# Two-layer message passing on a graph: dense rows moved out of the first 14 steps of stage one, and three node types packed into one number

## What is computed

```python
h = jnp.maximum(_layernorm(x, axis=-1), 0.0)
gate = jax.nn.silu(edge_attr @ W1.T + b1) @ W2.T + b2
ei = emb[atom_z[src]]
ej = emb[atom_z[dst]]
gate = gate + jnp.sum(ei * (ej @ adaptW.T), axis=-1, keepdims=True)
msg = gate * h[dst] * (cw * mj)[:, None]
agg = jax.ops.segment_sum(msg, src, num_segments=N)
tot = jax.ops.segment_sum(mj, src, num_segments=N)
x = x + layernorm(h + agg / jnp.clip(tot, 1e-08, None)[:, None]) * gamma + beta
```

## Time and profile before

| what | value |
|---|---|
| median of 3 runs | 1542.93 us (1542.01 to 1545.06) |
| the profiled execution's own time | 1533.91 us |
| its span in the trace | 1532.2 us |
| mean granted clock of PE | 0.598 |
| busy: PE, PEld, DVE, ACT, POOL | 76%, 55%, 87%, 40%, 67% |

### The profile page before, as it was taken

The page is one execution under the profiler, slowest core; times in us unless marked ns, Lnnn a source line. Parts: engine busy times, 40 slices in busy tenths (PEclk is TensorE's granted clock), DMA queues, the critical chain, the costliest instruction groups (busy, mean ns, idle before and its releaser), DMA issues.

```text
span 1532.2 us, 20105 instructions
## 1 busy us (share of the span) xinstructions
PE 1157.1 (76%) x5198; PEld 846.7 (55%) x5198; DVE 1336.7 (87%) x3937; ACT 618.2 (40%) x1423; POOL 1025.5 (67%) x809
## 2 busy tenths in 40 slices
PE   5898999989999989991047878888888888886000
PEld 2677777777777777771035555555555555554000
DVE  6999999999999999880299999999999999993598
ACT  2544444544445444440034444444444444442000
POOL 7655567777887676666537887887878878866100
PEclk9756555655556565555556565555655655557555
DMA  7999986666666566642446665555555555533899
GB/s 228 305 320 333 325 228 155 153 145 145 142 164 154 136 155 138 147 103 11 130 156 169 170 161 139 140 139 140 138 137 139 140 141 139 140 71 58 295 396 390
DMA packets 154389, 268.72 MB, mean 175 GB/s; under 512 B 73818, under 2 KB 90411, under 8 KB 153380
## 3 DMA queue, kind: packets, MB, share of 16 engines
q1 hardware_dynamic: 78228, 223.53, 43.5%
q0 software_dynamic: 68992, 24.64, 17.5%
q10 hardware_dynamic: 7056, 19.27, 3.1%
HBM read 194.33 MB, written 112.55 MB: 200 GB/s over the span
## 4 chain that ended last, share of the span: by engine, by line
PE 32%; DMA 20%; DVE 19%; POOL 15%; issue 11%; ACT 3%; SPq 1%; POOLq 0%; ACTq 0%; DVEq 0%
POOL agg L468 11%; PE ps_m L555 11%; DMA t<-agg,src_all 6%; PE ps_m L644 6%; PE ps_qs L555 4%; DMA agg<-x,once 3%; PE ps_k L630 3%; DMA lows<-low 2%; DVE x L1038 2%; DVE same L834 2%; DMA agg<-y,once 2%; DVE t L1042 2%; POOL nodes L426 2%; DMA agg<-ysq,once 2%; POOL agg L504 2%
## 5 line engine op out<-in xcount | busy, mean ns | idle before, releaser
L504 POOL DMA_INDIRECT agg<-sums,once x196 | 317.8, 1621 | 89.5 <-issue 64.1
L426 POOL DMA_INDIRECT nodes<-in_table,dst_all x196 | 194.1, 990 | 104.0 <-issue 50.2
L495 POOL DMA_INDIRECT t<-agg,src_all x196 | 190.3, 971 | 83.7 <-issue 49.1
L555 PEld LDWEIGHTS ps_m<-msg,same 128*128 128x128 f32 x980 | 200.4, 314 | 29.8 <-issue 29.8
L555 PE MATMUL ps_m<-msg,same 128*128 128x48 f32 x980 | 208.2, 398 | 1.0 <-issue 1.0
L630 PE MATMUL ps_k<-h_t,rw_sb 56*128 56x256 f32 x588 | 132.3, 571 | 96.3 <-ACT hid L724 73.7
L555 PEld LDWEIGHTS ps_qs<-msg,same 128*128 128x128 f32 x980 | 183.0, 288 | 2.1 <-DVE msg L926 2.1
L555 PE MATMUL ps_qs<-msg,same 128*128 128x49 f32 x980 | 180.1, 362 | 2.0 <-DVE msg L926 2.0
L468 POOL DMA_INDIRECT agg<-x,once x84 | 135.1, 1609 | 49.0 <-issue 21.9
L630 PEld LDWEIGHTS ps_k<-h_t,rw_sb 56*128 56x128 f32 x588 | 67.6, 260 | 144.6 <-ACT hid L724 100.6
L644 PE MATMUL ps_m<-hid,rw_sb 128*64 128x256 f32 x588 | 136.1, 634 | 0.0
(11 more groups left out here) (149 smaller groups left out, 2575.1 us busy)
## 6 DMA issues: line engine op xcount, KB each, us to landing
agg<-in_both SPq DMA_DIRECT2D x14, 2758.0 KB
t<-agg SPq DMA_DIRECT2D x49, 784.0 KB, 4.4
kept<-kept_out SPq DMA_DIRECT2D x49, 404.0 KB, 2.8
kept_in<-kept SPq DMA_DIRECT2D x49, 404.0 KB
agg<-bias_rows SPq DMA_DIRECT2D x49, 384.0 KB
out<-t ACTq DMA_DIRECT2D x49, 384.0 KB, 5.8
rows<-in_src_rows SPq DMA_DIRECT2D x49, 256.0 KB, 4.1
rows<-in_dst_rows SPq DMA_DIRECT2D x49, 256.0 KB, 3.2
```

The costliest lines, as they stand in the source:

```text
L426: pool.indirect_dma_start(nodes[s][:, t, :], None, table, bass.IndirectOffsetOnAxis(ap=dst_all[:, c:c + 1], axis=0)).then_inc(nodes_in[b % ...
L495: pool.indirect_dma_start(t2[b % T2S][:, t, :], None, wide, bass.IndirectOffsetOnAxis(ap=src_all[:, c:c + 1], axis=0)).then_inc(ends_in[b ...
L504: pool.indirect_dma_start(agg1, bass.IndirectOffsetOnAxis(ap=once1[b % LAG1][:, t:t + 1], axis=0), sums1[b % LAG1][:, t, :], None, compute ...
L555: last = mm(ps[:, t * width:(t + 1) * width], kept_same[:, at:at + P], m[:, v, :], start=(v == t), stop=(v == TILES - 1))
```

## The change

Two things are changed in stage one.

**Dense rows.** The first 14 steps (`DRY = FILLS`), those in which SP issues the fill, have no dense work. The 49 chunks are spread over the other 35 steps: `chunks_of(b)` gives one chunk to 21 steps and two chunks to 14 (b = 16, 18, 21, 23, ... 46, 48). The first chunk of a step ("mid") is done at the places of before, except that PE's `centred` for it now stands between the transposes and `sums0`. The second ("late") has places of its own: on DVE `dsum` and the reduction of `sqd` stand ahead of `glog`, the rest behind it; on PE `centred` stands behind `h1`. `dc` and `ps_c` are doubled. The standard deviations of the edges get tiles of their own (`evar0`, `estd0`), and POOL's early gathers follow `logit_done` in place of `pc_done`. Some constants and weights are loaded later.

**Packed types.** The 392 columns are cut into three classes of 131. Types of the three classes are scaled by 1, 128 and 16384 and summed in PSUM, so that a tile has six matmuls of 131 columns in place of two of 392, and DVE selects from 131 columns. Three small instructions on 4 elements (`unpack`, `open_type`, `keep_type`) convert, shift and mask the number.

```diff
+DRY = FILLS
+def chunks_of(b):
+    if b < DRY:
+        return []
+    left = NBLOCK - DRY
+    return list(range((b - DRY) * NBLOCK // left, (b + 1 - DRY) * NBLOCK // left))
...
 def lookup(b, t):
-                mm(ps_l[t % 2], low_hot[:, 0, t * P:(t + 1) * P], types_lo[:, 0, :], start=True, stop=False)
-                mm(ps_l[t % 2], low_hot[:, 1, t * P:(t + 1) * P], types_lo[:, 1, :], start=False,
-                   stop=True).then_inc(S["low_done"], 1)
+                for k in range(2):
+                    for c in range(PACK):
+                        last = mm(ps_l[t % 2], low_hot[:, k, t * P:(t + 1) * P], types_lo[:, k, c, :],
+                                  start=(k == 0 and c == 0), stop=(k == 1 and c == PACK - 1))
+                last.then_inc(S["low_done"], 1)
...
 (PE, step b)
                 last.then_inc(S["turned_t_done"], 1)
+                for c in chunks_of(b)[:1]:
+                    if c + 1 < NBLOCK:
+                        centred(c + 1)
                 if b > 0:
                     sums0(b - 1)
...
                 if b + 1 < NBLOCK:
                     h1(b + 1)
-                    centred(b + 1)
+                if b == DRY - 1:
+                    centred(0)
+                for c in chunks_of(b)[1:]:
+                    if c + 1 < NBLOCK:
+                        centred(c + 1)
...
 (ACT, step b)
+                for c in chunks_of(b - 1)[1:] + chunks_of(b)[:1]:
+                    dense_std(c)
                 act.wait_ge(S["var_e_done"], b + 1)
-                act.wait_ge(S["var_d_done"], b + 1)
-                need(act, kept_stored[b % 2], 16 * (b // 2))
-                A(kept_out[b % 2][:, PC:PC + G], kept_out[b % 2][:, PC + G:KEPT], ACT.Sqrt, bias=eps[:, :], scale=1.0 / H).then_inc(S["std_done"], 1)
+                need(act, S["rstd_done"], b)
+                A(estd0[:, :], evar0[:, :], ACT.Sqrt, bias=eps[:, :], scale=1.0 / H).then_inc(S["std_done"], 1)
                 if b + 1 < NBLOCK:
                     gate_hidden(b + 1)
-                    hidden(b + 1)
+                if b == DRY - 1:
+                    hidden(0)
+                for c in chunks_of(b):
+                    if c + 1 < NBLOCK:
+                        hidden(c + 1)
...
 (DVE)
+            def dense_var(c):
+                dve.wait_ge(S["kept_set"], 2)
+                dve.wait_ge(S["sqd_done"], c + 1)
+                need(dve, kept_stored[c % 2], 16 * (c // 2))
+                V.tensor_reduce(kept_out[c % 2][:, PC + G + TILES:KEPT], sqd[c % 2][:, :, :], AX_X, ALU.add).then_inc(S["var_d_done"], 1)
...
+                for c in late:
+                    if c + 1 < NBLOCK:
+                        dense_sum(c + 1)
+                    dense_var(c)
                 dve.wait_ge(S["logit_done"], b + 1)
                 dve.wait_ge(S["gate_done"], b + 1)
                 V.tensor_tensor(glog[:, :, :], ps_gate.rearrange("p (t h) -> p t h", h=H), cols(logit[:, :], H), ALU.add).then_inc(S["glog_done"], 1)
+                for c in late:
+                    if c + 1 < NBLOCK:
+                        dense_centre(c + 1)
+                    dense_mean(c)
+                if b + 1 < NBLOCK:
+                    unpack(b + 1)
...
+                if b + 1 < NBLOCK:
+                    open_type(b + 1)
+                for c in late:
+                    dense_out(c)
```

More of the change, by code:

```diff
@@ L40 @@
 assert NHI * LO == NP
+PACK = 3
+HW = -(-NHI // PACK)
+BITS = 7
+assert NTYPE <= 1 << BITS and BITS * PACK < 24
 CW1 = NREL * H
@@ L63 @@
 POOL_SET = 15
-CONSTS = 13
+CONSTS = 8
+LATE = 5
+DRY = FILLS
[4 more added lines that the diff above has]
+    return list(range((b - DRY) * NBLOCK // left, (b + 1 - DRY) * NBLOCK // left))
+assert sum((chunks_of(b) for b in range(NBLOCK)), []) == list(range(NBLOCK))
+assert max(len(chunks_of(b)) for b in range(NBLOCK)) == 2 and len(chunks_of(DRY)) == 1
 def place(t):
@@ L247, in build @@
         ps_c = ps_k[0]
-        ps_l = [ps_k[1][:, a, 0:NHI] for a in range(2)]
+        ps_l = [ps_k[1][:, a, 0:HW] for a in range(2)]
         ps_h1 = ps_m[0:H, :]
@@ L475, in _ @@
                 gather(FIRST + 2 * step)
-                pool.wait_ge(S["pc_done"], step + 1)
+                pool.wait_ge(S["logit_done"], step + 1)
                 gather(FIRST + 2 * step + 1)
@@ L569, in _ @@
                 lookup(0, t)
-            centred(0)
             for b in range(NBLOCK):
@@ L677, in _ @@
             gate_hidden(0)
-            hidden(0)
             for b in range(NBLOCK):
@@ L781, in _ @@
             dve.wait_ge(S["types_in_done"], 16)
-            V.tensor_copy(types_lo[:, :, :].rearrange("p k n -> p (k n)"), types_in[:, :])
+            for c in range(PACK):
+                V.tensor_scalar(types_lo[:, :, c, :], types_in[:, :, c, :], float(1 << (BITS * c)), None, ALU.mult)
             dve.wait_ge(S["idx_in"], 32)
@@ L803, in _ @@
             V.tensor_tensor(cw_a[:, :], cw_all[:, :], cw_b[:, :], ALU.max).then_inc(S["vec_set"], 1)
+            for s in range(2):
+                V.memset(kept_out[s][:, PC:KEPT], 0.0).then_inc(S["kept_set"], 1)
             def low_masks(b):
@@ L821, in _ @@
                 type_of(0, t)
+            unpack(0)
+            open_type(0)
+            keep_type(0)
             dve.wait_ge(S["act_set"], 3)
@@ L892, in _ @@
                     type_of(b + 1, 1)
-                    dense_centre(b + 1)
-                dve.wait_ge(S["rsum_done"], b + 1)
-                V.scalar_tensor_tensor(out=kept_out[s][:, 0:PC].rearrange("p (r f) -> p r f", r=NR), in0=cols(rsum[:, :], H),
-                                       scalar=-1.0 / H, in1=rl[s][:, :, :], op0=ALU.mult, op1=ALU.add).then_inc(S["pc_done"], 1)
+                for c in mid:
+                    dense_out(c)
                 dve.wait_ge(S["std_done"], b + 1)
-                V.reciprocal(rstd[:, :], kept_out[s][:, PC:PC + TILES]).then_inc(S["rstd_done"], 1)
+                V.reciprocal(rstd[:, :], estd0[:, :]).then_inc(S["rstd_done"], 1)
                 dve.wait_ge(S["q_done"], b + 1)
-                dve.wait_ge(S["zsel_done"], (b + 1) * TILES)
+                dve.wait_ge(S["zs_done"], b + 1)
                 for t in range(TILES):
@@ L912, in _ @@
                     type_of(b + 1, 3)
+                if b == DRY - 1:
+                    dense_sum(0)
+                    dense_centre(0)
+                if b == 2:
+                    dve.wait_ge(S["late_in"], 16 * LATE)
+                    V.tensor_copy(bias_rows[:, :, :], each(rb2_b[:, :], NR)).then_inc(S["vec_set"], 1)
+                for c in late:
+                    if c + 1 < NBLOCK:
+                        dense_sum(c + 1)
+                    dense_var(c)
                 dve.wait_ge(S["logit_done"], b + 1)
```

181 lines of the change are left out of this document (122 added, 59 removed).

## The result

The changed kernel took 1605.93 us (median of four runs, 1590.37 to 1626.21) beside 1543.99 for the kernel before on the same chip. The ratio is 1.0378, with a 95% interval of 1.0300 to 1.0457: slower. A second set of runs (experiment 8) had a median of 1603.82 and gave 1.0327 (1.0270 to 1.0384). The ratios leave out runs over 1.5% above the fastest of their kernel, one of four here and two of four in the second set; the medians of all runs stand at 1.040 and 1.041. The forecast was 1593. The profiled execution took 1590.37 (span 1588.7), 56.5 us more than that of before.

The account below looks back on a forecast made before the run. A loop through PE and DVE was taken to set low-clock steps, with POOL ending stage one. Steps +91, small items -2.0 and +1.8, POOL's tail -39.8 gave +51 on 1542.93: 1593 us, range 1530 to 1640.

Parts of the forecast that it names:

- two-chunk steps behind ACT's squares: DVE's late reduction of `sqd` waits for ACT's `hidden` behind `gate_hidden`, so `glog` starts at 18.0 at the low clock.
- Empty steps: Fill steps b = 0 to 13 without dense work: 14.0 us low clock, 10.8 raised, mean 12.6, together 176.
- The moved loads and stores on SP, the gathers behind `logit_done`, and the doubled `dc` cost nothing: Small items in stage one, claimed to cost nothing as long as a step is above 10 us.
- share of raised steps: Share of steps in which the clock rises, 0.45 (22 of 49) from the trace, kept for all kinds of step.
- The low loop of 14.0: Empty step at the low clock: the loop through PE and DVE stays, 11.58 + 2.38 + 0.07 for `unpack`.
- One-chunk steps: 21 steps with `centred` ahead of `sums0`: 15.9 us low clock, 12.8 raised, mean 14.5, together 304.
- Two-chunk steps: 13 steps among the 48: 22.6 us low clock, 17.4 raised, mean 20.3, together 264.
- Lookups at no change: On PE, 24 pairs of 131 columns replace 8 of 392 at no change, a load hiding beside a matmul.
- the other bound of the range (+27): Lookups' loads don't hide: +1.0 in each of some 27 low steps, 1620 us; rival's chance 0.15.
- POOL: POOL starts adds near 198 and catches up, so the tail after the last copy shrinks 48.8 to 9.0: -39.8.
- The sum: Stage one in total: +91 steps, -2.0 before the first, +1.8 in the last, -39.8 POOL's tail: +51 us.

Follow-up runs that it names:

- experiment 8: The changed kernel run once more without edits, beside the others on one chip: 1603.82 us, ratio 1.0327.
- experiment 1: Changed kernel with ACT squaring the first late chunk ahead of the gate's hidden layer in two-chunk steps: 1585.5 us, ratio 1.0274.
- experiment 9: Changed kernel with its seven new semaphores named at the end of the list, on a second chip: 1573.77 us, ratio 1.0284.
- experiment 2: Changed kernel with POOL's second gather of the first 14 steps waiting for `q_done` instead of `logit_done`: 1588.36 us, ratio 1.0306.
- 6: Changed kernel with POOL's second gather of a fill step at `ec_done`, eight gathers in one row: 1625.66 us, ratio 1.0538.
- 7: Changed kernel with the 14 fill pieces issued two a step in steps 7 to 13: 1625.77 us, ratio 1.0571.
- experiment 10: Changed kernel with dense rows not moved, POOL's old wait for `pc_done`, and constants, weights and bias loaded ahead of the fill: 1551.51 us, ratio 1.0124.
- 12: Changed kernel with new semaphores last, ACT's late squares ahead of the gate's hidden layer, and POOL's second gather behind `q_done`: 1561.72 us, ratio 1.0173.
- 3: Changed kernel with packing undone (392 columns again), dense rows still moved: 1616.21 us, ratio 1.0477.
- 4: Changed kernel with dense rows not moved, one chunk in every step and `centred` at its old place: 1580.94 us, ratio 1.0247.
- 5: Changed kernel with dense rows not moved and POOL's second gather behind `pc_done` again: 1576.04 us, ratio 1.0255.

## Why the forecast was right, and where not

The verdict and the size were right, and the largest step, two-chunk steps behind ACT's squares, is shown by the rows and by experiment 1. That the sum of the steps came within 2 us was luck: a cost that nobody forecast, the late signals, made up for two terms that this execution had below their price. Point by point:

- **Empty steps** (forecast 176, measured 217.7). Two parts. The late signals of PE cost some 31 us, 217.7 less the 186.7 of experiment 9 (on another chip); no step of the forecast had them. "The moved loads and stores on SP, the gathers behind `logit_done`, and the doubled `dc` cost nothing" is the sentence that failed: with the gathers behind `q_done` instead the same steps took 202.4 (experiment 2), against 217.7 and 215.3 (experiment 8, the same chip). What the moved loads cost isn't shown. The other 11 us (13.3 a step in experiment 9, instead of 12.6) are the share of raised steps: only 2 of 14 had the short form of 11.0 to 11.3. The low loop of 14.0 was right.
- **One-chunk steps** (304, measured 286.1; 288.0 in experiment 9, 294.9 in 8). Both kinds were right within a microsecond: at the low clock 15.0 (priced 15.9), raised 12.6 (12.8). `centred` hid partly, and the share of raised steps was above 0.45.
- **Two-chunk steps** (264, measured 238.9). Priced 22.6 and 17.4, measured 20.9 to 21.4 and 17.0 to 17.5. The share of short ones was 9 of 13 here, and 6, 4, 7, 4 and 6 of 13 in experiments 2, 6, 7, 8 and 9, which have the same order of work in these steps: 36 of 78 or 0.46, the 0.45 taken. Long ones took 20.7 to 22.9 there, and the 13 steps 251.5, 263.6, 249.6, 264.3 and 249.2. So the term was priced well, and low in this one execution. One such step more or less at the low clock is 4 us. This is a good part of why the changed kernel's runs lie 1590 to 1626 apart: the profiled execution of experiment 8 is 24.6 us longer than this one, and its two-chunk steps are 25.4 longer.
- **Lookups at no change**: right. Twelve pairs take 1.30 us at the low clock (134.21 to 135.51 in the fill step above) against 1.28 for the four long matmuls before (404.37 to 405.65, where the transposes start, the row below), so the other bound of the range (+27) is out. At the raised clock twelve pairs take 0.81 (484.34 to 485.15), 0.07 each, against 0.76. The selection of 131 columns costs 345 ns (worked out as 0.34).

```profile
405.65 1.06 PE L578 MATMUL ps_t<-ident,onehot 128*119 128x128 f32 x4
```

- **POOL** (-39.8): the gap from last copy to stage two went from 48.8 to 14.8, so -34.0. Its adds did not begin early as forecast (198), but late (242.3), so it had not caught up. Where it had, in experiments 8 and 9, the gap is 9.8, against 9.0 forecast.
- **The sum**: steps +89.5, first one-hot -0.8, from the last one-hot to the last copy +2.8, tail -34.0, together +57.5; the span grew by 56.5.

What the 56.5 us consist of, by spans of profiled executions: before 1532.2; with packing, split root and opened types but nothing moved 1539.9 (experiment 10), **+8**, from POOL's slower adds; with the dense rows moved and no late signals 1561.1 (experiment 9), **+21**; with late signals 1588.7, **+28**. These are single executions and not all on one chip. The timed ratios, each against the kernel before on its own chip, split the loss otherwise: 1.24% or 19 us for experiment 10, 1.6% or some 25 us more for 9, and only 0.4 to 0.9% or some 7 to 15 us more for the changed kernel. So the size of the first and the third step in an average run stays open.

Why the move can't pay is shown by one comparison: 14 steps of the fill take 189.5 us with the dense rows in them (before) and 186.7 without (experiment 9). In the fill the dense rows are all but free. Outside it a two-chunk step takes 18.4 (changed kernel) to 19.2 us (experiment 9), 20.3 in experiment 8, against 13.6 for a step of before: 4.8 to 6.7 more, and there are 13.

**What stays open** is the cause of the late signals. Nine profiles have them (the changed kernel and experiments 1 to 8) and five don't (the kernel before and 9 to 12), and two things separate the groups besides the edits. One is the chip: 1 to 8 ran on one, 9 to 12 on two others, on which neither the changed kernel nor another version with late signals was run. The other is the profile itself. Each transfer issued has 16 updates of its semaphore when it lands, 23,136 in all. The five clean profiles hold 22,400 to 22,526 of these records, the nine others only 13,302 to 14,353, and they lack them after 800 us too, where the change alters nothing and no signal is late. In the list of transfers the last number is the median time to landing, and it stands only where no record of the semaphore is missing. This is the load of `agg` in stage two, in the changed kernel and in experiment 9:

```profile
t<-agg SPq DMA_DIRECT2D x49, 784.0 KB
...
t<-agg SPq DMA_DIRECT2D x49, 784.0 KB, 4.5
```

So the chip, or how it was recorded there, is a rival to both edits that seemed to remove the late signals, the place of the semaphores (9) and the loads ahead of the fill (10), and no run separates them; the changed kernel on the chip of 9 would. That it is the chip alone is unlikely: the kernel before, timed on the chip of experiments 1 to 8, took 1540 to 1543 against 1534 on the others, 7 to 9 us more and not 28.

What the runs on one chip do show: the late signals don't need the fill's traffic (7), the short pairs of PE (3) or the moved dense rows (4, 5), and with another wait for POOL's gathers other signals are hit (2, 5, 6). They were seen only in the stretch with rows of gathers, but the profiles of the kernel before and of experiment 9 have the same rows of gathers and none of them.

The Trainium skill ("Perfetto Trace Analysis", Tensor Engine Instruction) says that PE pushes a semaphore's update only when PSUM has acknowledged the write, that the update then has to spread to the other engines, and that the profile's end time holds neither. The trace agrees that such a tail is outside PE's rows: from the end of the sums to ACT's start it is normally 0.03 us here (160.50 to 160.53), and in the bad case 2.4. No run here tells acknowledgement from spreading.

## What to carry to other kernels

Before work is moved out of a stretch that looks crowded, measure what that stretch takes without it: here two engines were 90% busy and the dense rows still cost 3 us of 190. When several chunks share a step, put the work that a queue's head waits for first; with two chunks behind one gate, each position is a wait. And when an edit seems to remove an idle time that the profile ascribes to nothing, run the unedited kernel again on the same chip beside it: here the edits and the chip changed together, and what the two best-looking experiments removed can't be told.

## What was unexpected of the hardware

- Signals of PE reached ACT and DVE 1.5 to 3.8 us late, once 10.9 (25.91 to 36.83), in nearly every step of the fill. The updates of the semaphores were themselves recorded late, two of them 0.05 apart for groups that ended 1 us apart (103.81 and 103.86 for 101.12 and 102.10). The waits ended 2.0 to 2.8 us after a gather's start in the steady steps (143.15 after 140.75; 103.88 and 103.91 after 101.84).
- The nine profiles with late signals hold some 60% of the landing records (13,302 to 14,353 of 23,136), the five without 97% (22,400 to 22,526). The two go together without exception; which of them causes the other, or whether the chip is behind both, no run shows.
- A clock that rises more often isn't a gain by itself: the changed kernel's stretch from 400 to 600 us ran at 0.72 instead of 0.61, with PE busy 147.56 us of 200 where it had been busy 185.22; its steps were longer all the same.
